# Two attentions of a fused two-layer block: the mixes of the key tiles one chunk sooner on TensorE, and their copy on ScalarE behind chunk 3

## The chip, the cores and the metric

One core of one Trainium2 chip runs the whole program in one launch. The metric is the time of an execution on the device in microseconds, as the median of several runs.

## What is computed

The reference is a block of two layers on x of shape (8, 512, 128). Each layer normalises x and adds an attention and a feed-forward branch to it. The change touches only the two attentions, which have 16 heads of 8 dimensions and a causal mask:

```
scores = q @ k^T            (layer 0: q_cos k_cos + q_sin k_sin, scaled by a factor of the head)
scores = where(causal mask, scores, -inf)
attn   = softmax(scores, axis=-1)
out    = (attn @ v) @ Wo.T
```

## The kernel before

The program runs in phases: setup, mix0, middle0, attend0, middle1, experts1, attend1. attend0 and attend1 are the same function, `attend` (line 1863 on), with layer 0 or 1.

**Units.** The work of an attention is cut into 32 units: 8 batches (called rows) by 4 groups of 4 heads. A unit is one batch's 512 queries against its 512 keys for 4 heads. The causal mask leaves four key tiles of 128 (kt 0 to 3) with 512, 384, 256 and 128 queries each.

**Steps.** Each engine has a program of its own and walks through steps t = 0, 1, 2, ... (`in_steps`). In step t TensorE has in hand:
- unit t: `maxima`, the scores with queries on the partitions, from which VectorE takes each query's maximum (`reduce`);
- unit t-1: `turn_maxima`, which turns the maxima round, so that VectorE can copy them (`copy_maxima`) and SyncE's DMA can put them into q as extra rows;
- unit t-2: `probabilities`, the scores with keys on the partitions, less the maximum, which ScalarE takes to exponentials (`exponentials`, line 2089) and GpSimd masks on the diagonal (`mask`, line 2052);
- unit t-3: `mix` (line 2176), the exponentials times the values. It runs once for each key tile in the order 0, 1, 3, 2, with 4 heads side by side as 32 columns each of the array (shape 128*32), and adds up in one bank, MIX. ScalarE copies the bank to mixT (line 2114);
- unit t-4: `turn_mix` (line 2184), which turns mixT in four pieces of 128*128 into the bank TURN, from where VectorE divides by the sums (`divide`, lines 2287 and 2291) into context.

A step has five chunks, c = 0 to 4, because the scores of a unit fill five pairs of banks. In each chunk TensorE issues the probabilities of side 0, the maxima, and the probabilities of side 1; all three use the array as two halves of 64 partitions (shapes 50*128, 48*128 and 64*128). The probabilities have one bank a side: those of chunk c wait until ScalarE has taken the exponentials of chunk c-1 of that side. `maxima` has two pairs of banks and waits for the reduction two chunks back.

**What stands between the chunks on TensorE.** After chunk 0 `turn_mix`. After chunk 1 the mix of tile 0 and `turn_maxima`, which waits for the divided context, since both use the bank TURN. After chunk 2 the mix of tile 1. After chunk 3 the mixes of tiles 3 and 2. When the unit t-4 was the last of a row, there are also `turn_context` after chunk 2 (line 2190) and `project` after chunk 4 (line 2196), the copy of the turned context on ScalarE after chunk 3's exponentials (line 2102), and the sum into x on VectorE (`add_row`, lines 2304 and 2308), for which the next `turn_mix` waits.

**Other engines.** ScalarE's step is the ten exponentials in order, then the copy of the mix. VectorE's step is `split_maxima` of unit t-1 (lines 2271 and 2273), then the five reductions (lines 2255, 2258, 2260, 2261) with `divide` after the first and `copy_maxima` after the second. GpSimd gathers rows by DMA, copies the values (line 2060) and masks. In attention 0 it also has the second norm of the other branch, with products at lines 2022, 2027 and 2031, and in attention 1 the additions at line 2041. In attention 0 the norm adds statistics on VectorE in one step of four and four activations on ScalarE (line 2107) in the next. The order is written out by hand in the `step` functions, and semaphores carry the waits.

## Time and profile before

| | us |
|---|---|
| median of 3 runs | 1272.88 |
| lowest and highest of them | 1272.55, 1272.88 |
| the profiled execution | 1268.47 |
| its span | 1266.9 |
| busy TensorE (matmul), share of the span | 981.7, 77% |
| busy VectorE | 819.4, 65% |
| busy ScalarE | 690.9, 55% |
| busy GpSimd | 582.5, 46% |
| line 2089, exponentials, 640 of 600 ns | 351.1 |
| line 2176, mixes, 2048 instructions | 178.9 |

The profile records one execution. A row of its timeline has the start from the beginning of the span, the length, the engine, the line of the kernel, the operation, what is written and read, the shapes, and in brackets the idle time in front of it with the instruction that ended it. PE is TensorE, PEld its weight loads, ACT ScalarE, DVE VectorE, POOL GpSimd. Rows that follow on each other with the same form are merged (x4). A matmul's length has a tail that overlaps with the next one, so distances between starts tell more than lengths do. Attention 0 runs from about 395 to 660 us of the span, and attention 1 from about 1000 to its end.

### The profile page before, as it was taken

To read this page: it belongs to the slowest core of one execution; us is meant where nothing else is said; L and a number is where in the kernel's file an instruction comes from. 1 tells how busy PE (TensorE), PEld (TensorE's weight loads), DVE (VectorE), ACT (ScalarE), POOL (GpSimd) and SP (SyncE) were. 2 spreads that over 40 slices of the span, in tenths; PEclk is the share of its full clock that TensorE was granted. 3 is DMA by queue.
4 is the path that set the end of the run, shared out by engine and by line. 5 is a ranking of instruction groups with operands and counts; after the bars stand their busy time and mean duration, and the time that the engine had idled before them with its cause. 6 is when DMAs were issued, how large, how long until landed. Compare 5 with 4: busy or idle time off the path is not lost. (4 is left out here: it accounts for less than half of the span.)

```text
span 1266.9 us, 27743 instructions
## 1 busy us (share of the span) xinstructions
PE 981.7 (77%) x8908; PEld 647.1 (51%) x8908; DVE 819.4 (65%) x1770; ACT 690.9 (55%) x1325; POOL 582.5 (46%) x793
## 2 busy tenths in 40 slices
PE   3789652989867988888872655199999599999987
PEld 1456431777753544444431433188888345555553
DVE  1566341667748999999943776133333699999992
ACT  1366343878714777677763454022222277777775
POOL 3467537010112565565551466411110367777775
PEclk9899776999985999999996666599999599999999
DMA  4321042577752222222201434456665112211111
GB/s 134 108 51 51 26 118 74 160 210 225 208 172 77 80 69 69 72 76 62 73 24 36 115 115 119 142 164 194 185 192 163 39 46 54 55 52 51 51 45 30
DMA packets 151735, 126.30 MB, mean 100 GB/s; under 512 B 23760, under 2 KB 134272, under 8 KB 151648
## 3 DMA queue, kind: packets, MB, share of 16 engines
q1 hardware_dynamic: 141904, 107.05, 29.5%
q0 software_dynamic: 8016, 17.71, 4.8%
q8 instruction: 44, 0.72, 0.2%
q10 hardware_dynamic: 1728, 0.46, 0.2%
q14 instruction: 43, 0.35, 0.1%
HBM read 77.83 MB, written 44.70 MB: 97 GB/s over the span
## 5 line engine op out<-in xcount | busy, mean ns | idle before, releaser
L2089 ACT ACTIVATE attend_probs<-attend_attend_ps 128x512 f32<-128x512 f32 x640 | 351.1, 600 | 161.7 <-PE attend_attend_ps L2163 154.4
L2163 PE MATMUL attend_attend_ps<-attend_q,attend_ks 50*128 50x512 f16 (+3 forms) x1024 | 236.5, 307 | 20.1 <-ACT attend_probs L2089 18.0
L2052 POOL TENSOR_SCALAR_AFFINE_SELECT attend_probs<-attend_probs 128x512 f32<-128x512 f32 x256 | 158.7, 637 | 159.5 <-ACT attend_probs L2089 158.6
L2131 PE MATMUL attend_attend_ps<-attend_ks,attend_q 48*128 48x512 f16 (+3 forms) x1024 | 191.3, 317 | 25.5 <-DMA attend_ks<-k_stack 16.2
L2176 PE MATMUL attend_attend_ps<-attend_probs,attend_vals 128*32 128x512 f32 (+3 forms) x2048 | 178.9, 446 | 0.0
L2258 DVE TENSOR_REDUCE attend_neg_max<-attend_attend_ps 128x2 f32<-128x1024 f32 x128 | 155.0, 1211 | 9.9 <-PE attend_attend_ps L2143 9.8
L2143 PE MATMUL attend_attend_ps<-identb,stairs 64*128 64x128 bf16 (+1 forms) x1280 | 144.3, 213 | 0.0
L2163 PEld LDWEIGHTS attend_attend_ps<-attend_q,attend_ks 50*128 50x128 f16 x1024 | 70.9, 94 | 116.1 <-ACT attend_probs L2089 93.2
L2260 DVE TENSOR_REDUCE attend_neg_max<-attend_attend_ps 128x2 f32<-128x768 f32 x128 | 121.8, 951 | 9.2 <-PE attend_attend_ps L2143 8.4
L1800 DVE TENSOR_TENSOR experts_hidden<-experts_experts_ps,experts_gate 128x512 f32<-128x512 f32 x39 | 27.0, 691 | 136.3 <-ACT experts_gate L1779 136.3
L2143 PEld LDWEIGHTS attend_attend_ps<-identb,stairs 64*128 64x128 bf16 x1280 | 105.9, 100 | 17.5 <-issue 4.7
L1834 PE MATMUL experts_experts_ps<-experts_rowsT,experts_w_in 128*128 128x256 f32 (+1 forms) x468 | 110.1, 385 | 1.6 <-ACT experts_rowsT L1787 1.5
L1104 POOL DMA_INDIRECT sorted<-middle_scaled,rank_row x64 | 66.6, 1040 | 58.1 <-issue 28.9
L1834 PEld LDWEIGHTS experts_experts_ps<-experts_rowsT,experts_w_in 128*128 128x128 f32 (+1 forms) x468 | 82.4, 183 | 17.6 <-ACT experts_rowsT L1787 2.1
L1779 ACT ACTIVATE experts_gate<-experts_experts_ps 128x512 f32<-128x512 f32 x39 | 23.3, 597 | 120.8 <-PE experts_experts_ps L1834 120.8
L1766 POOL DMA_DIRECT2D experts_rows<-sorted x39 | 27.7, 712 | 131.8 <-issue 131.8
L2131 PEld LDWEIGHTS attend_attend_ps<-attend_ks,attend_q 48*128 48x128 f16 x1024 | 67.2, 96 | 39.0 <-DMA attend_ks<-k_stack 16.6
L2255 DVE TENSOR_REDUCE attend_neg_max<-attend_attend_ps 128x4 f32<-128x1024 f32 x64 | 78.3, 1224 | 8.5 <-PE attend_attend_ps L2143 8.5
L1430 POOL TENSOR_TENSOR x_sum<-middle_amp_n,middle_sine 128x1024 f32<-128x1024 f32 x8 | 18.9, 2365 | 118.4 <-DVE middle_amp_n L1636 118.3
L2068 POOL DMA_INDIRECT attend_moe<-done,back_row x64 | 61.6, 962 | 14.9 <-issue 14.9
L1846 PE MATMUL experts_experts_ps<-experts_w_out,experts_hidden 128*128 128x128 f32 (+1 forms) x468 | 58.7, 275 | 0.9 <-DVE experts_result L1811 0.9
L2176 PEld LDWEIGHTS attend_attend_ps<-attend_probs,attend_vals 128*32 128x32 f32 x2048 | 44.7, 109 | 22.8 <-issue 5.9
(319 smaller groups left out, 1950.7 us busy)
## 6 DMA issues: line engine op xcount, KB each, us to landing
experts_w_in<-in_L_ffn_w_dram SPq DMA_DIRECT2D x78, 176.0 KB, 2.4
q_stack<-middle_parts SPq DMA_DIRECT2D x24, 256.0 KB, 3.3
k_stack<-middle_parts SPq DMA_DIRECT2D x24, 256.0 KB, 3.6
attend_q<-q_stack SPq DMA_DIRECT2D x64, 96.0 KB, 2.2
attend_ks<-k_stack SPq DMA_DIRECT2D x64, 96.0 KB, 2.2
middle_w_in<-in_L_ffn_W_dram SPq DMA_DIRECT2D x23, 256.0 KB, 2.7
middle_w_out<-in_L_ffn_W_dram SPq DMA_DIRECT2D x23, 256.0 KB, 3.1
experts_rows<-sorted POOLq DMA_DIRECT2D x39, 128.0 KB, 2.5
```

The source lines that it names most:

```text
L1104: pool.indirect_dma_start(k.sorted1, bass.IndirectOffsetOnAxis(ap=k.rank_row[:, c * NT + tile:c * NT + tile + 1], axis=0), scaled[:, c, ti ...
L1834: mm = pe.matmul(ps[0:size[c], hidden_bank(u, bank), half * ROWS:(half + 1) * ROWS], w_in[:, u.phase, w + c * P:w + c * P + size[c]], rows ...
L2052: pool.affine_select(out=block_, in_=block_, compare_op=ALU.is_ge, fill=0.0, base=0, pattern=[[0, GH], [1, P]], channel_multiplier=-1).the ...
L2068: pool.indirect_dma_start(moe[:, c * NT + n, :], None, src, bass.IndirectOffsetOnAxis(ap=at_row[:, c * NT + n:c * NT + n + 1], axis=0))\
L2089: act.activation(probs[:, u.par, 2 * c + side, :], ps[:, PROB + side, :], ACT.Exp, scale=SCALE ** -2)\
L2131: pe.matmul(ps[:, bank + side, col:col + (qt + 1) * P], q[rows(side, KR), g, pair, qt * P:(qt + 1) * P], ks[rows(side, KR), g, pair, 0:(qt ...
L2143: mm = pe.matmul(span[:, :, col:col + 64], k.stairs[here, stair:stair + P], k.identb[here, here].unsqueeze(1).broadcast_to([64, len(blocks ...
L2163: mm = pe.matmul(ps[:, PROB + side, col:col + S - kt * P], ks[rows(side, KM), g, pair, kt * P:(kt + 1) * P], q[rows(side, KM), g, pair, kt ...
L2176: mm = pe.matmul(ps[32 * h:32 * h + 32, MIX, kt * P:S], vals[:, u.par, kt * GH + h, :], probs[:, u.par, 2 * c + h % 2, col:col + S - kt * ...
L2255: ins = dve.tensor_reduce(out[:, :, :, 1], pair_banks.rearrange("p s (h t) -> p s h t", h=HP), X_AXIS, ALU.max, negate=True)
L2258: ins = dve.tensor_reduce(out[:, :, c // 2, 3], pair_banks, X_AXIS, ALU.max, negate=True)
L2260: dve.tensor_reduce(out[:, :, c // 2, 2], pair_banks[:, :, 0:384], X_AXIS, ALU.max, negate=True)
```

## The change

On TensorE the mix of tile 0 moves from behind chunk 1 to behind chunk 0, ahead of `turn_mix`. The mix of tile 1 moves from behind chunk 2 to behind chunk 1, ahead of `turn_maxima`, and those of tiles 3 and 2 move from behind chunk 3 to behind chunk 2, ahead of `turn_context`. On ScalarE the copy of the mix moves from the end of the step to behind chunk 3's exponentials, ahead of the copy of the turned context and of chunk 4's exponentials. Its waits are the same. The number of instructions is the same.

```diff
--- before.py
+++ after.py
@@ -2095,6 +2095,12 @@
                     if active(t, 2, UNITS):
                         for side in range(2):
                             exponentials(t - 2, c, side)
+                    if c == 3 and active(t, 3, UNITS):
+                        u = t - 3
+                        act.wait_ge(mixed.sem, mixed.done(u))
+                        if u.past(1):
+                            act.wait_ge(mix_turned.sem, mix_turned.done(u - 1))
+                        act.copy(mixT[:, :], ps[:, MIX, :]).then_inc(mixT_ready.sem, 1)
                     if c == 3 and row_ends:
                         r = (t - 4).row
                         act.wait_ge(context_turned.sem, context_turned.done(r))
@@ -2106,12 +2112,6 @@
                         for j in range(QT):
                             act.activation(z_norm[:, j, :], z_sum[:, j, :], ACT.Identity, bias=z_shift[:, j:j + 1],
                                            scale=z_rstd[:, j:j + 1]).then_inc(z_normed.sem, 1)
-                if active(t, 3, UNITS):
-                    u = t - 3
-                    act.wait_ge(mixed.sem, mixed.done(u))
-                    if u.past(1):
-                        act.wait_ge(mix_turned.sem, mix_turned.done(u - 1))
-                    act.copy(mixT[:, :], ps[:, MIX, :]).then_inc(mixT_ready.sem, 1)
 
             in_steps(act, UNITS, DEPTH + 1 - layer, step, 2 * NG, 2 * NG)
 
@@ -2222,13 +2222,13 @@
                         maxima(t, c)
                     if active(t, 2, UNITS):
                         probabilities(t - 2, c, 1)
+                    if active(t, 3, UNITS) and c <= 2:
+                        mix(t - 3, c)
+                        if c == 2:
+                            mix(t - 3, 3)
                     if c == 0 and active(t, 4, UNITS):
                         before_mix(t)
                         turn_mix(t - 4)
-                    if 1 <= c <= 3 and active(t, 3, UNITS):
-                        mix(t - 3, c - 1)
-                        if c == 3:
-                            mix(t - 3, 3)
                     if c == 1 and active(t, 1, UNITS):
                         before_maxima(t)
                         turn_maxima(t - 1)
```

## Rows read from the trace of the kernel before

**Rows 1.** Windows, attention 0: us, then PE, PEld, DVE, ACT, POOL busy; clock; DMA.
```profile
411.00:640.00 229.00, 199.09 (x2553) 109.11 (x2548) 218.11 (x401) 173.54 (x336) 132.81 (x196) 1.00 0.25 70
```

**Rows 2.** Timeline of TensorE, attention 1, one step: start us, length us.
```profile
1120.43 0.33 PE L2163 MATMUL attend_attend_ps<-attend_q,attend_ks 50*128 50x384 f16 x1
...
1121.10 0.86 PE L2176 MATMUL attend_attend_ps<-attend_probs,attend_vals 128*32 128x128 f32 x16
1121.89 0.28 PE L2163 MATMUL attend_attend_ps<-attend_q,attend_ks 50*128 50x256 f16 x1
...
1122.96 0.39 PE L2163 MATMUL attend_attend_ps<-attend_q,attend_ks 50*128 50x512 f16 x1 [0.34 <-ACT attend_probs L2089]
...
1123.45 0.39 PE L2163 MATMUL attend_attend_ps<-attend_q,attend_ks 50*128 50x512 f16 x1
1124.02 0.63 PE L2184 MATMUL attend_attend_ps<-ident,attend_mixT 128*128 128x128 f32 x4 [0.18 <-ACT attend_mixT L2114]
1124.58 0.39 PE L2163 MATMUL attend_attend_ps<-attend_q,attend_ks 50*128 50x512 f16 x1
...
1124.93 0.38 PE L2163 MATMUL attend_attend_ps<-attend_q,attend_ks 50*128 50x512 f16 x1
...
1125.24 1.07 PE L2176 MATMUL attend_attend_ps<-attend_probs,attend_vals 128*32 128x512 f32 x8
1126.12 0.22 PE L2151 MATMUL attend_attend_ps<-identh,attend_max_parts 128*32 128x128 f16 x1
1126.27 0.33 PE L2163 MATMUL attend_attend_ps<-attend_q,attend_ks 50*128 50x384 f16 x1
...
1126.88 0.85 PE L2176 MATMUL attend_attend_ps<-attend_probs,attend_vals 128*32 128x384 f32 x8
1127.67 0.33 PE L2163 MATMUL attend_attend_ps<-attend_q,attend_ks 50*128 50x384 f16 x1
```

**Rows 3.** Timeline of ScalarE, attention 1: the same step.
```profile
1122.31 1.09 ACT L2089 ACTIVATE attend_probs<-attend_attend_ps 128x512 f32<-128x512 f32 x2 [0.37 <-PE attend_attend_ps L2163]
1123.28 0.59 ACT L2114 COPY attend_mixT<-attend_attend_ps 128x512 f32<-128x512 f32 x1
1123.75 2.34 ACT L2089 ACTIVATE attend_probs<-attend_attend_ps 128x512 f32<-128x512 f32 x4
```

**Rows 4.** Timeline of ScalarE, attention 1: further copies of the mix.
```profile
1106.44 0.59 ACT L2114 COPY attend_mixT<-attend_attend_ps 128x512 f32<-128x512 f32 x1
...
1115.22 0.61 ACT L2114 COPY attend_mixT<-attend_attend_ps 128x512 f32<-128x512 f32 x1
...
1130.52 0.59 ACT L2114 COPY attend_mixT<-attend_attend_ps 128x512 f32<-128x512 f32 x1
```

**Rows 5.** Timeline of ScalarE, attention 0: copies of the mix.
```profile
548.68 0.59 ACT L2114 COPY attend_mixT<-attend_attend_ps 128x512 f32<-128x512 f32 x1
...
557.72 0.59 ACT L2114 COPY attend_mixT<-attend_attend_ps 128x512 f32<-128x512 f32 x1
...
565.92 0.59 ACT L2114 COPY attend_mixT<-attend_attend_ps 128x512 f32<-128x512 f32 x1
```

**Rows 6.** Timeline of VectorE, attention 0, beside GpSimd.
```profile
558.60 1.20 DVE L2273 SCALAR_TENSOR_TENSOR attend_max_parts<-attend_neg_max,attend_max_parts 128x16 f16<-128x16 f32 x1
...
561.14 0.29 DVE L2291 TENSOR_TENSOR attend_context<-attend_attend_ps,attend_inv 128x128 f32<-128x128 f32 x1
```

**Rows 7.** Timeline of GpSimd, attention 0, at that moment.
```profile
558.50 1.27 POOL L2027 TENSOR_TENSOR attend_z_gain<-attend_z_norm,row 128x512 f32<-128x512 f32 x1
```

**Rows 8.** Timeline of TensorE, attention 0, a step that ends a row.
```profile
536.50 0.85 PE L2176 MATMUL attend_attend_ps<-attend_probs,attend_vals 128*32 128x384 f32 x8
537.28 0.66 PE L2190 MATMUL attend_attend_ps<-ident,attend_context 128*128 128x128 f32 x4
...
539.98 1.16 PE L2196 MATMUL attend_attend_ps<-wT,attend_contextT 128*128 128x128 f32 x8
```

**Rows 9.** Waits, attention 0, 450 to 630 us: total us, times, longest us.
```profile
PE attend_attend_ps L2151 <- DVE attend_context L2291: 14.8, 14, 1.4
```

## Prediction

> **What bounds the kernel now.** I read four views in this order: the windows, to see which engine is full in the attentions; TensorE's timeline of one step, to see what follows what; ScalarE's timeline of the same step, to see what TensorE waits for; and then the copies of the mix (line 2114, one a step), whose distances are the lengths of the steps. The change touches both attentions and nothing else, so only the 31 steps of each in which score matmuls and mixes run together count.
>
> In attention 0 VectorE is busy 218.11 of 229.00 us, 95%, at a granted TensorE clock of 1.00, full speed [rows 1]. That looks like the bound. TensorE's timeline says that it is only a near neighbour. Call the start of chunk 3's first probability matmul zero (1120.43). Then chunk 4's comes at 1.46, the next step's chunk 0 at 2.53, its second side at 3.02, the turning of the mix at 3.59, chunk 1 at 4.15 and its second side at 4.50, mix of key tile 0 at 4.81, the turning of the maxima at 5.69, chunk 2 at 5.84, the second mix at 6.45 and zero again at 7.24 [rows 2]. Two places in this line are waits. Chunk 0 stands 0.34 idle for an exponential, and the turning of the mix stands 0.18 idle for the copy of the mix. Everywhere else one piece of TensorE follows on another.
>
> ScalarE's side of it [rows 3]: chunk 4's first exponential starts at 1122.31, which is 0.42 after its matmul (1121.89), and chunk 0's matmul (1122.96) starts 0.65 after that exponential. So each side needs 0.42 + 0.65 = 1.07 us for a chunk, whatever TensorE's load is, since each side has one bank. Two exponentials take 0.97 (to the copy at 1123.28) and the copy holds back what is behind it by 0.47 (1123.75). One loop sets the step: TensorE's pieces from chunk 0's second side to chunk 4, and then the round trip over ScalarE.
>
> The steps' lengths: an ordinary one takes 7.24 (1123.28 to 1130.52), the one after a row's last unit 8.06 (1115.22 to 1123.28), the one into it in attention 1 8.78 (1106.44 to 1115.22) [rows 3, 4]. In attention 0 two steps of each row are long, 9.04 and 8.20 [rows 5]. In the 8.20 step VectorE's second half of the split maxima takes 1.20 and ends at 559.80, 0.03 after a GpSimd product that runs from 558.50 to 559.77, and the context is only there at 561.43 [rows 6, 7].
>
> **The edit on ScalarE.** The copy moves from behind chunk 4 to behind chunk 3. Its own wait, for the mix, costs nothing, because the last mix now stands ahead of chunk 3's probability matmuls on TensorE. Behind it in ScalarE's queue stand chunk 4's exponentials. Chunk 3's first exponential starts at 0.42, the copy at 0.42 + 0.97 = 1.39, chunk 4's exponentials at 1.86 and 2.35, and so chunk 0's matmuls at 1.86 + 0.65 = 2.51 and 3.00. Before they came at 2.53 and 3.02. The 0.79 us of the last two mixes that leave chunk 3 (1121.10 to 1121.89 [rows 2]) therefore buy nothing: what they occupied, the copy and the round trip of 1.07 now occupy. At the other end the copy is done long before the turning of the mix, which removes the wait of 0.18 there.
>
> **The edit on TensorE.** At 3.00 the old order had 0.57 to the turning of the mix. The new one puts the first mix there. The steps of the sum:
> - second side of chunk 0 to the mix: 0.31, as chunk 1's second side to the mix now (1124.93 to 1125.24); mix at 3.31.
> - mix of key tile 0: 0.88 to the turning of the maxima (1125.24 to 1126.12), which has the mix's shape (128*32). Leaving for another shape costs more: the second mix has 384 columns of 512, three quarters, which of 0.88 is 0.66, and takes 0.79 to chunk 3's matmul [rows 2]. So a change of shape is an estimated 0.13. The same 384-column mix takes 0.78 to the turning of the context [rows 8], so turning counts as another shape, and the first mix costs 0.88 + 0.13 = 1.01 here. Turning of the mix at 4.32, chunk 1 0.56 later at 4.88.
> - chunk 1 takes 0.66 to its mix (1124.58 to 1125.24), the second mix 0.66 because the maxima are turned behind it, and these 0.15: chunk 2 at 6.35.
> - chunk 2 takes 0.61, the last two mixes 0.79: zero again at 7.75.
>
> The ordinary step goes from 7.24 to 7.75, **+0.51**. Put shortly: one mix piece enters chunk 0 where only 0.26 was slack, and what leaves chunk 3 was covered. The change of shapes saved is in this sum: from mix to turning is still a change of shape, so of eight changes a step seven are left, and it gives 0.13. The Trainium skill, "TensorEngine Tiling (Array Packing)", Key Properties, says that changing the tiling mode drains TensorE; with the 0.13 the trace agrees. Read as the thing that bounds the step, that rule would make the edit a gain, and the rows' price for it is rival (a).
>
> VectorE can follow, since its work stays the same, 95% of the old steps' time, and the steps get longer. The turning of the maxima waits for the divided context. With the mix turned at about 4.9 and 0.6 for the division (0.29 is its second half [rows 6]), it is there at 5.5, before 6.20.
>
> **The step behind a row's last unit.** ScalarE now has two copies in chunk 3: mix at 1.39, context at 1.86, ready at 2.45. The projection starts at 2.5 and takes 1.1 (1.16 with its tail [rows 8]), so chunk 0 starts at 3.6. Then 0.66 to the mix, 1.01, 0.56, 0.66, 0.66, 0.15, 0.61, 0.79: 8.70 against 8.06, **+0.64**. The turning used to wait there for VectorE's addition to the row; the first mix now covers that, and it is in the sum.
>
> **The long steps.** In the 8.20 step TensorE waits for the context at 561.43. The copy at 557.72 is 2.85 behind zero (1123.28 less 1120.43), so the context is at 6.56. The work that delays it hangs on chunk 4's last exponential, which does not move (2.35 against 2.36). New and old order both stand at 6.56 there, and 0.08 + 0.15 + 0.61 + 0.79 more give 8.2: **+0.0**. The 8.78 step is of this kind plus the turned context, and gains or loses nothing either. The 9.04 step waits for the context too: TensorE stood 14.8 us in 14 such waits, up to 1.4 each, in 180 us [rows 9]. There the masks come late, and the first mix may stand for one at chunk 0. I bound this step by −0.1 and +0.5 and take 0, since the long wait covers it.
>
> **Sum.** Attention 0, a row of four steps: 0.51 + 0.64 = 1.15. Attention 1: 2 × 0.51 + 0.64 = 1.66. Seven full rows each give 8.1 + 11.6 = 19.7, and the three steps at either attention's edges, at an estimated 0.3 each, 1.8: together +21.5. The profiled execution took 1268.47, with a span of 1266.9, so its successor would take 1290. The median of the runs, 1272.88, lies 4.4 above it; forecast **1294**.
>
> **Rivals.**
> (a) Faster. The ordinary step loses a change of shape (0.13) and the wait of 0.18 at the turning, and the first mix runs in the shadow of the exponentials. Then some 46 steps of the 62 that are not held by the context gain 0.31: −14, 1259. It decides at chunk 0: its second side must then be issued some 0.5 earlier than now. For it: the 0.13 itself, and two waits that go. Against: the copy in chunk 3 keeps chunk 0 at 2.51. Chance 0.06.
> (b) Nothing measurable. The wait for the context, which hides the edit in the 8.20 step, hides it everywhere; VectorE's 95% speaks for it in attention 0, and the missing wait ahead of the maxima's turning at 1126.12 against it in attention 1. About 1273. Chance 0.07.
> (c) Much slower, by a new collision. The division follows the turning that now comes 0.7 later, and VectorE's small operations fall on other GpSimd work. One took 1.20 [rows 6]. One more such collision per row, at the whole of it, is 16 × 1.2 = 19 on top: 1313. It decides if a division or a split meets a product that it misses now. The Trainium skill, "SBUF — State Buffer", Who interferes with whom, says that the loser of the shared ports blocks until the other instruction has finished; the 0.03 us between the two ends agrees. Chance 0.10.
> (d) The forecast's own mechanism, 0.77. That the edit does nothing can't be: both queues' orders change.
>
> Within 0.2% of the median (2.5 us, about what a measurement of this kernel tells from none) lies only (b): same 0.07, faster 0.06, slower 0.77 + 0.10 = 0.87. If attention 0 hides all of its 9.0 us and attention 1 pays two thirds of its 12.5, the time is about 1281; (c) but for its last microsecond gives the upper end. Range 1279 to 1312.
>
> **What would show it.** Right: the copy of the mix 1.4 behind chunk 3's start, chunk 4's exponential straight behind it with no idle time, chunk 0's matmuls at 2.5 and 3.0, about 1.0 from first mix to turning, ordinary steps of 7.7 to 7.8 and the 8.20 steps unchanged. Wrong: ordinary steps under 7.3, chunk 0 before 2.2, or a mix that waits on masks in ordinary steps.

## Result and profile after

The changed kernel takes 1302.29 us, the median of 5 runs (1300.51 to 1304.25), against 1272.59 for the kernel before beside it (5 runs, 1271.64 to 1272.88): a ratio of 1.0237, 95% interval 1.0223 to 1.0251, slower by 30 us. Forecast were 1294 in a range of 1279 to 1312. The profiled execution took 1302.29 as well; that of the kernel before, 1268.47, is faster than all five of its runs, so the two profiles differ by more than the medians do.

The profile's page, part 1: the span and the engines' busy time.

```profile
span 1300.7 us, 27743 instructions
...
PE 1005.9 (77%) x8908; PEld 654.7 (50%) x8908; DVE 830.5 (64%) x1770; ACT 690.5 (53%) x1325; POOL 582.0 (45%) x793
```

The instruction counts are those of before. The span has grown by 33.8 us, from 1266.9. TensorE's busy time grew with it by 24 us (from 981.7), and that has to be explained, since the work is the same.

TensorE's timeline in an ordinary step of attention 1, to be laid beside [rows 2]. Columns: start, length, engine, line, operation, idle time in front.

```profile
1152.99 0.33 PE L2163 MATMUL attend_attend_ps<-attend_q,attend_ks 50*128 50x384 f16 x1
...
1154.07 0.28 PE L2163 MATMUL attend_attend_ps<-attend_q,attend_ks 50*128 50x256 f16 x1 [0.34 <-ACT attend_probs L2089]
...
1155.54 0.39 PE L2163 MATMUL attend_attend_ps<-attend_q,attend_ks 50*128 50x512 f16 x1 [0.59 <-ACT attend_probs L2089]
...
1156.03 0.39 PE L2163 MATMUL attend_attend_ps<-attend_q,attend_ks 50*128 50x512 f16 x1
1156.35 1.07 PE L2176 MATMUL attend_attend_ps<-attend_probs,attend_vals 128*32 128x512 f32 x8
1157.34 0.66 PE L2184 MATMUL attend_attend_ps<-ident,attend_mixT 128*128 128x128 f32 x4
1157.93 0.39 PE L2163 MATMUL attend_attend_ps<-attend_q,attend_ks 50*128 50x512 f16 x1
...
1158.59 0.85 PE L2176 MATMUL attend_attend_ps<-attend_probs,attend_vals 128*32 128x384 f32 x8
1159.26 0.22 PE L2151 MATMUL attend_attend_ps<-identh,attend_max_parts 128*32 128x128 f16 x1
1159.41 0.33 PE L2163 MATMUL attend_attend_ps<-attend_q,attend_ks 50*128 50x384 f16 x1
...
1160.02 0.86 PE L2176 MATMUL attend_attend_ps<-attend_probs,attend_vals 128*32 128x128 f32 x16
1160.81 0.33 PE L2163 MATMUL attend_attend_ps<-attend_q,attend_ks 50*128 50x384 f16 x1
```

Zero of the prediction, chunk 3's first probability matmul, is at 1152.99. Counted from there: chunk 4 at 1.08, chunk 0 at 2.55 and its second side at 3.04, the first mix at 3.36, the turning at 4.35, chunk 1 at 4.94, the second mix at 5.60, the turning of the maxima at 6.27, chunk 2 at 6.42, the last mixes at 7.03, zero again at 7.82. The prediction had 1.07, 2.51, 3.00, 3.31, 4.32, 4.88, 5.54, 6.20, 6.35, 6.96 and 7.75. Two places now are long waits for exponentials, 0.34 at chunk 4 and 0.59 at chunk 0. The waits for the copy and behind it are gone, and between chunk 0 and chunk 3 TensorE never waits.

ScalarE in the same step, beside [rows 3].

```profile
1153.42 1.08 ACT L2089 ACTIVATE attend_probs<-attend_attend_ps 128x512 f32<-128x512 f32 x2 [0.31 <-PE attend_attend_ps L2163]
1154.39 0.59 ACT L2103 COPY attend_mixT<-attend_attend_ps 128x512 f32<-128x512 f32 x1
1154.86 2.19 ACT L2089 ACTIVATE attend_probs<-attend_attend_ps 128x512 f32<-128x512 f32 x4
...
1162.20 0.59 ACT L2103 COPY attend_mixT<-attend_attend_ps 128x512 f32<-128x512 f32 x1
```

The copy starts 1.40 after zero (1154.39), chunk 4's first exponential straight behind it at 1154.86, and the next copy comes 7.81 later. This is the ordinary step, 7.24 before.

The steps' lengths, as distances of the copies (attention 0 unless said otherwise; "behind" and "into" leave out the edges of the attentions):

| step | before | after | forecast |
|---|---|---|---|
| ordinary | 7.24 | 7.82 | 7.75 |
| into the row's last unit, attention 0 | 7.82 | 8.40 | as ordinary, +0.51 |
| behind a row's last unit, attention 1 | 7.86 to 8.06, mostly 7.98 to 8.02 | 8.68 | 8.70 |
| behind a row's last unit, attention 0 | 7.87 to 7.97; 10.07 and 9.76 at the start of two turns of the loop | 8.68; 10.75 and 8.68 there | 8.70 |
| with the norm's activations | 9.02 to 9.12 | 9.05 to 9.07, twice 10.56 | 9.04 |
| with GpSimd's products | 8.20 | 8.21, twice 9.33 | 8.20 |
| into the last unit, attention 1 | 8.78 | 8.81 | 8.78 |

From the first copy to the last, attention 0 takes 267.5 us where it took 250.9, and attention 1 252.0 where it took 236.1. These 32.4 us are all but 1.4 of the span's growth. The last distance of attention 0 alone grew from 3.72 to 5.46, at a clock of 0.69; the kernel before has the same in its second trace (5.41 at 0.68, further down), so the change is not its cause.

The 9.07 step kept its length because its wait for the context absorbed the first mix. TensorE at the turning of the maxima in it, in the kernel before and in the changed one:

```profile
485.12 0.23 PE L2151 MATMUL attend_attend_ps<-identh,attend_max_parts 128*32 128x128 f16 x1 [1.36 <-DVE attend_context L2291]
```

```profile
490.46 0.23 PE L2151 MATMUL attend_attend_ps<-identh,attend_max_parts 128*32 128x128 f16 x1 [0.32 <-DVE attend_context L2291]
```

Of 1.36 us of waiting 0.32 are left. Ahead of the first mix TensorE now waits 0.19 for a mask, as the prediction had thought possible.

What the forecast lacked are above all the steps of 10.56 and 9.33. The windows of the changed kernel, with these steps as stretches: us, busy PE, PEld, DVE, ACT, POOL, then TensorE's granted clock.

```profile
520.96:531.52 10.56, 9.39 (x93) 4.25 (x91) 9.13 (x19) 7.32 (x16) 5.53 (x9) 0.74 0.27 76
531.52:540.85 9.33, 8.39 (x93) 4.08 (x90) 8.41 (x13) 5.90 (x12) 6.26 (x8) 0.82 0.20 57
557.93:568.49 10.56, 8.92 (x94) 4.13 (x91) 9.14 (x19) 7.38 (x17) 5.53 (x9) 0.84 0.28 76
...
593.78:602.85 9.07, 7.60 (x94) 3.75 (x91) 8.93 (x19) 7.32 (x16) 5.56 (x9) 1.00 0.31 88
```

The long steps have a mean clock of 0.74, 0.82 and 0.84; an undisturbed 9.07 step (the last row) has 1.00. Between 411 and 650 us of the span the mean is 0.96, where the kernel before has 1.00 ([rows 1], to 640 us). TensorE's timeline in the third of these steps shows the lower of the two levels, 1.2 GHz in place of 2.4, in the instructions' lengths.

```profile
559.08 0.39 PE L2163 MATMUL attend_attend_ps<-attend_q,attend_ks 50*128 50x512 f16 x1 [0.59 <-ACT attend_probs L2089]
...
560.42 1.83 PE L2176 MATMUL attend_attend_ps<-attend_probs,attend_vals 128*32 128x512 f32 x8 [0.17 <-POOL attend_probs L2052]
562.19 1.11 PE L2184 MATMUL attend_attend_ps<-ident,attend_mixT 128*128 128x128 f32 x4
```

The first mix takes 1.83 where it takes 1.07 in the ordinary step, and the turning 1.11 in place of 0.66. Part of TensorE's additional busy time is there. The granted clock in this step is 1.00 up to 560 us and 0.50 from 561 to 564. Just before it fell, TensorE had stood 0.34 us for chunk 4's exponential (557.61) and 0.59 for chunk 0's (559.08), 0.9 us together, where it stands 0.34 in the kernel before. It is so at nearly every fall: this trace and a second one of the changed kernel (below) have eleven falls before the last distances of the attentions, and ten of them come right behind such a wait of 0.59 to 0.68 us in chunk 0, at most 1.5 us after it. The eleventh, between 519 and 520 us, came behind a wait of 1.59 us for the context (517.72); the kernel before waits 1.41 at the same place (511.15) and keeps 1.00. Idle time added up over a step does not explain it: the norm's step of the kernel before has TensorE busy for 7.07 of 9.05 us, that of the changed kernel for 7.57 of 9.07.

### The profile page after: what moved, and what is told of

It is laid out like the page before. It is cut to its first block and busy times, and to the rows that moved or that the text cites. A ratio compares the mean times of both kernels' runs of the same rounds, so it can differ in the third digit from the quotient of the medians.

```text
span 1300.7 us, 27743 instructions
## 1 busy us (share of the span) xinstructions
PE 1005.9 (77%) x8908; PEld 654.7 (50%) x8908; DVE 830.5 (64%) x1770; ACT 690.5 (53%) x1325; POOL 582.0 (45%) x793
## 5 line engine op out<-in xcount | busy, mean ns | idle before, releaser
L2163 PE MATMUL attend_attend_ps<-attend_q,attend_ks 50*128 50x512 f16 (+3 forms) x1024 | 241.1, 309 | 54.1 <-ACT attend_probs L2089 51.3
L2131 PE MATMUL attend_attend_ps<-attend_ks,attend_q 48*128 48x384 f16 (+3 forms) x1024 | 187.8, 317 | 24.5 <-DMA attend_ks<-k_stack 16.3
L2176 PE MATMUL attend_attend_ps<-attend_probs,attend_vals 128*32 128x512 f32 (+3 forms) x2048 | 184.9, 457 | 1.2 <-POOL attend_probs L2052 0.9
L2143 PE MATMUL attend_attend_ps<-identb,stairs 64*128 64x128 bf16 (+1 forms) x1280 | 140.7, 214 | 0.0
L2143 PEld LDWEIGHTS attend_attend_ps<-identb,stairs 64*128 64x128 bf16 x1280 | 102.0, 100 | 19.2 <-issue 5.0
L2131 PEld LDWEIGHTS attend_attend_ps<-attend_ks,attend_q 48*128 48x128 f16 x1024 | 63.5, 96 | 37.4 <-DMA attend_ks<-k_stack 16.7
```

The source lines that it names most:

```text
L2131: pe.matmul(ps[:, bank + side, col:col + (qt + 1) * P], q[rows(side, KR), g, pair, qt * P:(qt + 1) * P], ks[rows(side, KR), g, pair, 0:(qt ...
L2143: mm = pe.matmul(span[:, :, col:col + 64], k.stairs[here, stair:stair + P], k.identb[here, here].unsqueeze(1).broadcast_to([64, len(blocks ...
L2163: mm = pe.matmul(ps[:, PROB + side, col:col + S - kt * P], ks[rows(side, KM), g, pair, kt * P:(kt + 1) * P], q[rows(side, KM), g, pair, kt ...
L2176: mm = pe.matmul(ps[32 * h:32 * h + 32, MIX, kt * P:S], vals[:, u.par, kt * GH + h, :], probs[:, u.par, 2 * c + h % 2, col:col + S - kt * ...
```

## Experiments

Each kernel was compared with the kernel before on its own chip, so ratios carry over from one group to the next and medians don't.

### One edit at a time

Only ScalarE's edit:

```diff
@@ scalar, step(t)
+                    if c == 3 and active(t, 3, UNITS):
+                        ...
+                        act.copy(mixT[:, :], ps[:, MIX, :]).then_inc(mixT_ready.sem, 1)
...
-                if active(t, 3, UNITS):
-                    ...
-                    act.copy(mixT[:, :], ps[:, MIX, :]).then_inc(mixT_ready.sem, 1)
```

> Only ScalarE's edit is made: the copy of the mix stands behind chunk 3's exponentials, the mixes stay behind chunks 1, 2 and 3. The round-trip theory: the copy now has to wait for the mixes behind chunk 3 and starts about 1.65 us after the chunk's start, so chunk 4's exponential comes at 2.13 in place of 1.88 and chunk 0 of the next step 0.25 later; but the 0.26 us in which the turning of the mix waited for the copy go, so an ordinary step stays at 7.24 (7.2 to 7.3). In the step that ends a row the copy of the context slips behind the copy of the mix, the projection starts some 0.7 later, and the 8.06 steps become 8.6 to 8.8. Sum about +9 us, 1280 to 1284. The rival, that the early copy is what costs in the changed kernel, wants ordinary steps of 7.6 and over, and 1290 or more.

Ratio 1.014 (1.0104 to 1.0176). TensorE in an ordinary step of attention 0, where zero is 421.14:

```profile
421.14 0.33 PE L2163 MATMUL attend_attend_ps<-attend_q,attend_ks 50*128 50x384 f16 x1
...
423.95 0.37 PE L2163 MATMUL attend_attend_ps<-attend_q,attend_ks 50*128 50x512 f16 x1 [0.63 <-ACT attend_probs L2089]
...
424.68 0.65 PE L2184 MATMUL attend_attend_ps<-ident,attend_mixT 128*128 128x128 f32 x4
...
425.92 1.06 PE L2176 MATMUL attend_attend_ps<-attend_probs,attend_vals 128*32 128x512 f32 x8
426.94 0.23 PE L2151 MATMUL attend_attend_ps<-identh,attend_max_parts 128*32 128x128 f16 x1
```

Chunk 0 is at 2.81 and the turning at 3.54 (2.53 and 3.59 before), as the walk had it, with no wait at the turning. The step is 7.36 and not 7.24, because the turning of the maxima now starts 1.02 behind the first mix, not 0.88. The cause is VectorE's split of the maxima: its first half starts at 424.72, takes 0.31 and ends 0.02 behind GpSimd's last mask (424.37 and 0.64 long), and the reduction and the division stand behind it. In the steps behind a row's last unit the expected 8.6 to 8.8 came out as 8.56. Attention 0 as a whole takes 255.5 from first to last copy, 4.6 more than before, about half of the 9 that were expected of both attentions together. Its 8.20 steps rose to 8.40, which was not expected, and the 9.76 step behind a row's last unit fell to 8.73. No full step of attention 0 is at the lower clock.

In the group of these first four experiments attention 1 was slow in every kernel, in steps that end a row above all (10.2 us and more), and the kernel before took 1292.04 beside them. All four ratios are larger than expected (+18, +30, +18 and -11 us, where +9, +14 to +18, +8 to +14 and -2 to -5 were forecast). So I read their ratios for the sign, and the steps in attention 0 alone. The traces show one part of the slowness: with only ScalarE's edit the steps behind a row's last unit in attention 1 take 11.1 to 11.3 us at a clock of 0.69 to 0.70. What made the steps of 10.2 was not found; in the next group they were gone, on the same chip.

Only TensorE's edit:

```diff
@@ tensor, step(t)
+                    if active(t, 3, UNITS) and c <= 2:
+                        mix(t - 3, c)
+                        if c == 2:
+                            mix(t - 3, 3)
                     if c == 0 and active(t, 4, UNITS):
                         before_mix(t)
                         turn_mix(t - 4)
-                    if 1 <= c <= 3 and active(t, 3, UNITS):
-                        mix(t - 3, c - 1)
-                        if c == 3:
-                            mix(t - 3, 3)
```

> Only TensorE's edit is made: the mixes stand behind chunks 0, 1 and 2, the copy stays at the end of ScalarE's step. The round-trip theory: chunk 4's exponential comes at 1.49 after chunk 3's start, chunk 0 at 2.14 and 2.63, but the first mix then waits for the copy of the mix before (one bank), which ends at 3.07, and starts at 3.17. Ordinary steps of 7.63 to 7.70, the 8.06 steps 8.3, the 8.20 and 8.78 steps as before: 1286 to 1290. The rival, that fewer changes of shape on TensorE are worth something by themselves, wants ordinary steps at or under 7.24.

Ratio 1.0234 (1.0204 to 1.0264).

```profile
423.43 0.33 PE L2163 MATMUL attend_attend_ps<-attend_q,attend_ks 50*128 50x384 f16 x1
...
424.51 0.28 PE L2163 MATMUL attend_attend_ps<-attend_q,attend_ks 50*128 50x256 f16 x1 [0.35 <-ACT attend_probs L2089]
...
425.68 0.37 PE L2163 MATMUL attend_attend_ps<-attend_q,attend_ks 50*128 50x512 f16 x1 [0.29 <-ACT attend_probs L2089]
...
426.64 1.07 PE L2176 MATMUL attend_attend_ps<-attend_probs,attend_vals 128*32 128x512 f32 x8 [0.17 <-ACT attend_mixT L2114]
...
431.11 0.33 PE L2163 MATMUL attend_attend_ps<-attend_q,attend_ks 50*128 50x384 f16 x1
```

From zero at 423.43, chunk 4 is at 1.08, chunk 0 at 2.25, the first mix at 3.21 after an idle 0.17 for the copy, which is the one-bank wait of the expectation. The step is 7.68 (copies 7.67 apart). The steps behind a row's last unit came out as 7.85 and not 8.3, for which I had not walked through the earlier chunk 0. Those into a row's last unit rose by more than the ordinary ones, from 7.82 to 8.60, and the 8.20 steps fell to 7.95, where no change was expected; both stayed unexplained. TensorE's edit makes +0.43 of an ordinary step, ScalarE's +0.12, both +0.58. The rival, that fewer changes of shape are a gain, falls here. Chunk 0 at 2.25 also shows what the copy does in the changed kernel: with it behind chunk 3, chunk 0 comes at 2.55. This trace has two full steps of attention 0 at the lower clock (10.42 at 0.84 and 9.25 at 0.82) and one at its end (9.90 at 0.83); that of ScalarE's edit has none.

### Is the place that the last mixes leave worth anything?

```diff
-                    if 1 <= c <= 3 and active(t, 3, UNITS):
+                    if 1 <= c <= 2 and active(t, 3, UNITS):
                         mix(t - 3, c - 1)
-                        if c == 3:
+                        if c == 2:
+                            mix(t - 3, 2)
                             mix(t - 3, 3)
```

> Of the change only one part: the last two mixes go from behind chunk 3 to behind chunk 2, where the second mix already stands, so TensorE has one piece of mixes fewer per step, and the copy stays at the step's end. The round-trip theory: 0.66 us of mixes come in where TensorE is the bound and only 0.39 come out, since chunk 4 cannot start before 1.07 after chunk 3: ordinary steps +0.27 or, if the turning still waits for its copy, a little less, 7.45 to 7.55; in all 1280 to 1286. The rival, that each change of shape saved is a gain, wants -0.13 per step and 1265.

Ratio 1.0136 (1.0102 to 1.017); ordinary steps of 7.59, 0.04 more than the top of the expectation.

```profile
422.84 1.50 PE L2176 MATMUL attend_attend_ps<-attend_probs,attend_vals 128*32 128x384 f32 x24
424.27 0.33 PE L2163 MATMUL attend_attend_ps<-attend_q,attend_ks 50*128 50x384 f16 x1
...
425.35 0.28 PE L2163 MATMUL attend_attend_ps<-attend_q,attend_ks 50*128 50x256 f16 x1 [0.34 <-ACT attend_probs L2089]
...
426.52 0.37 PE L2163 MATMUL attend_attend_ps<-attend_q,attend_ks 50*128 50x512 f16 x1 [0.29 <-ACT attend_probs L2089]
```

The mixes of chunk 2 take 1.43 to chunk 3 (422.84 to 424.27), 0.64 more than one alone, and chunk 4 comes 1.08 behind chunk 3 where it came 1.46 behind it. So 0.64 come in and 0.38 go out; 0.10 more come in because chunk 0 now follows chunk 4 by 1.17 and not by 1.07. Together they make the 0.35 of the step. One piece of mixes less per step is a loss. It is the round trip over ScalarE, 1.08, that sets the distance of these chunks once TensorE has less to do than that.

The other direction, the last mix in chunk 4:

```diff
                     if 1 <= c <= 3 and active(t, 3, UNITS):
                         mix(t - 3, c - 1)
-                        if c == 3:
-                            mix(t - 3, 3)
+                    if c == (3 if row_ends else 4) and active(t, 3, UNITS):
+                        mix(t - 3, 3)
```

> The opposite direction: the last mix (256 columns) goes one chunk later, from behind chunk 3 to behind chunk 4, where TensorE stands idle for 0.34 us, except in the steps that end a row. One more change of shape per step. The round-trip theory: TensorE's own line would allow 6.9 us; VectorE, which needs about 7.07 of the 7.24, becomes the bound, so ordinary steps of 7.07 to 7.15, the others unchanged: -2 to -5 us, 1268 to 1271. The rival, that a change of shape costs more than the place gives, wants ordinary steps of 7.3 and over.

Ratio 0.9912 (0.9884 to 0.994).

```profile
423.45 0.33 PE L2163 MATMUL attend_attend_ps<-attend_q,attend_ks 50*128 50x384 f16 x1
...
425.34 0.64 PE L2176 MATMUL attend_attend_ps<-attend_probs,attend_vals 128*32 128x256 f32 x8
425.91 0.39 PE L2163 MATMUL attend_attend_ps<-attend_q,attend_ks 50*128 50x512 f16 x1
...
430.55 0.33 PE L2163 MATMUL attend_attend_ps<-attend_q,attend_ks 50*128 50x384 f16 x1
```

The mix (425.34) lies in what was idle time, chunk 0 comes 2.46 behind zero (423.45) in place of 2.53, and zero again at 7.10. Ordinary steps are 7.09 apart. With this mix gone from chunk 3, chunk 4 comes 1.08 behind chunk 3 (424.53) and not 1.46, and the mix then fills the time to chunk 0. A change of shape more per step, and it is faster: what counts is where the piece stands. The steps behind a row's last unit fell too, to 7.7, and the 8.20 steps to 7.92, which I had not expected.

### The long steps

The prediction let the change cost nothing where VectorE's context is late because of GpSimd's products. VectorE in such a step of the changed kernel, attention 1:

```profile
1164.06 0.46 DVE L2271 TENSOR_SCALAR attend_max_parts<-attend_neg_max 128x16 f16<-128x16 f32 x1
1164.55 1.21 DVE L2273 SCALAR_TENSOR_TENSOR attend_max_parts<-attend_neg_max,attend_max_parts 128x16 f16<-128x16 f32 x1
...
1167.10 0.29 DVE L2291 TENSOR_TENSOR attend_context<-attend_attend_ps,attend_inv 128x128 f32<-128x128 f32 x1
```

The split's second half takes 1.21, the context is there at 1167.39, and TensorE turns the maxima at 1167.44. The split's first half takes 0.46 (0.19 in the kernel before, and in e5 below): GpSimd's last mask (1163.86, 0.64 long) now runs when VectorE comes to it, as in the kernel with ScalarE's edit alone.

GpSimd's products spread over successive steps, on the kernel before and on the changed one:

```diff
@@ gpsimd
                 if n < UNITS:
-                    for i in range(QT):
-                        mask(n, i)
-                if layer == 0 and n >= 7 and (n - 7) % NG == 0:
-                    second_gain((n - 7) // NG)
-                if layer == 1 and n >= NG and n % NG == 0:
-                    join_branches(n // NG - 1)
+                    mask(n, 0)
+                if layer == 0 and n >= 7 and (n - 7) % NG == 0:
+                    second_scale((n - 7) // NG)
+                if layer == 0 and n >= 8 and (n % NG == 0 or n == UNITS + NG - 1):
+                    second_shift(n // NG - 2 + (n % NG) // 3)
+                if layer == 1 and n >= 3 and n % NG != 2 and n <= UNITS + 1:
+                    join_branches((n - 3) // NG, (n - 3) % NG)
+                if n < UNITS:
+                    for i in range(1, QT):
+                        mask(n, i)
```

second_scale and second_shift are the two products of second_gain, and join_branches does one of its three additions per call; only the second and the third wait for the gathered rows.

> The kernel before once more, for its trace on the same chip as the other runs of this call. Ordinary steps of 7.24 in both attentions, the steps that meet GpSimd's products 8.20 in attention 0 and 8.78 in attention 1. If the chip of the first call alone was slower in attention 1, these hold here; if it is this chip too, the extra time shows in the step into a row's last unit of attention 1, which took 10.2 us and more in all four runs of that call.

The profiled execution took 1268.28; both expectations of the first kind hold: 7.23, 8.19 to 8.20 and 8.78 to 8.80. Its steps are those of the first trace to 0.02 us nearly everywhere; the largest exception is the last distance of attention 0, 5.41 at a clock of 0.68 in place of 3.72 at 1.00.

> The kernel before with GpSimd's row work (two products of the norm in attention 0, three additions in attention 1) taken from behind the masks and put one at a time behind the first mask of successive steps, where GpSimd stands idle. Theory of the long steps: VectorE's split maxima wait for a GpSimd product to end, the context is late by a microsecond, and TensorE waits for it. Then the 8.20 steps fall to 7.24 and the 8.78 steps to 7.8, some 15 of them: 1256 to 1260. Rival: the long steps are long for their own TensorE work, and stay as they are: 1272.

Median 1256.50, ratio 0.988 (0.9857 to 0.9902). VectorE and GpSimd where the 8.20 step was:

```profile
558.21 0.19 DVE L2277 TENSOR_SCALAR attend_max_parts<-attend_neg_max 128x16 f16<-128x16 f32 x1
558.43 0.20 DVE L2279 SCALAR_TENSOR_TENSOR attend_max_parts<-attend_neg_max,attend_max_parts 128x16 f16<-128x16 f32 x1
...
559.97 0.29 DVE L2297 TENSOR_TENSOR attend_context<-attend_attend_ps,attend_inv 128x128 f32<-128x128 f32 x1
```

```profile
553.50 1.29 POOL L2027 TENSOR_TENSOR attend_z_gain<-attend_z_norm,row 128x512 f32<-128x512 f32 x1
...
558.32 0.29 POOL L2062 COPY attend_vals<-v_all 128x128 f32<-128x128 f32 x1
...
561.03 1.28 POOL L2033 TENSOR_TENSOR attend_z_tile<-attend_z_gain,row 128x512 f32<-128x512 f32 x1
```

The products stand in GpSimd's idle time (553.50, 561.03), the split's halves take 0.19 and 0.20, and the step is 7.23. In attention 1 all 8.78 steps are 7.82. So the 8.20 and 8.78 steps were long by the wait for a GpSimd product, and it could be had back without touching TensorE. The 9.04 steps stay at 9.02 to 9.11: their late context has another cause, which no run isolated. One step at the end of attention 0 is at the lower clock here too (8.32 at 0.79, where the kernel before has 7.86).

> The changed kernel with the same GpSimd work spread. If the wait for the context hides the change's 0.59 us in the 8.20 and 8.78 steps, they become 7.8 and 8.4 here, no lower, and the distance to the kernel before with the same spread (e5) is larger than that of the changed kernel to the kernel before: about 0.55 us in each of the 15 steps more, 8 us. The changed kernel gains only some 6 us from the spread: 1294 to 1298. Rival: the change costs nothing in these steps for another reason, and both kernels gain the same 15 us.

Median 1298.66, ratio 1.0234 (1.0204 to 1.0265) to the kernel before. The steps are 7.80 and 8.40, no lower. Against e5 the distance is 42 us, where 30 lie between the two original kernels. Of the 12 more, 15 steps of 0.58 are 9. The rest may be steps at the lower clock, of which this trace has six (9.33, 10.57, 10.73 and 10.28 in attention 0, 9.97 and 9.99 in attention 1), but that was not separated. So the change does cost its 0.58 in each of these steps as soon as their cover is taken away. The 6 us that the changed kernel itself was to gain from the spread do not show: its ratio is 1.0234 with it and 1.0237 without.

### The lower clock

> The changed kernel once more beside the one with the filler, on the same chip: some 1300 to 1304 where the kernel before takes 1271 to 1273; one to five steps in its trace that are over a microsecond longer than the others of their kind, each in a stretch at the lower granted clock, and at other places than in the first trace.

Median 1304.83 (6 runs), ratio 1.026 (1.023 to 1.0291). The trace has six such long steps in attention 0, one more than expected. Three are the same steps as in the first trace (the two that follow the first step of the loop's second turn, and the norm's step of the next row), three are others. The window over attention 0:

```profile
411.00:650.00 239.00, 206.65 (x2475) 109.97 (x2475) 218.19 (x391) 169.19 (x329) 130.72 (x193) 0.96 0.24 67
```

> The changed kernel with two matmuls of 512 columns more in chunk 4 of each step but those that end a row, into the bank TURN, which nobody reads at that time. They fall into the time in which TensorE waits for chunk 4's exponentials (0.59 us idle, 0.43 us of work), so ordinary steps stay at 7.82, at most 7.9. Theory of the rest of the loss: the steps of 9.3 and 10.6 us are steps at the lower TensorE clock, granted after TensorE had stood idle more than in the kernel before; with the filler the granted clock is 1.00 through both attentions, those steps are 8.2 and 9.07, and the time falls by 3 to 6 us against the changed kernel. Rival: the long steps come from GpSimd or DMA, and stay.

```diff
                     if c == 4 and row_ends:
                         project(t - 4)
+                    elif c == 4 and active(t, 2, UNITS) and active(t, 1, UNITS):
+                        pe.wait_ge(maxT_ready.sem, maxT_ready.done(t - 1))
+                        for _ in range(2):
+                            pe.matmul(ps[:, TURN, :], k.identb[:, :], k.stairs[:, 0:128].unsqueeze(1).broadcast_to([P, 4, P]),
+                                      start=True, stop=True)
```

Ratio 1.0254 (1.0228 to 1.028): no gain in time, but not for the rival's reason. All steps with the norm are 9.05 to 9.07, all with the products 8.21 to 8.22, ordinary ones stay at 7.82, and each of them is at 1.00. But two steps behind a row's last unit took 14.20 and 14.56. The window of such a step and TensorE in it:

```profile
503.00:518.00 15.00, 10.99 (x110) 5.74 (x109) 9.85 (x15) 6.88 (x13) 4.33 (x6) 0.77 0.15 40
```

```profile
505.49 1.16 PE L2196 MATMUL attend_attend_ps<-wT,attend_contextT 128*128 128x128 f32 x8 [0.58 <-ACT attend_contextT L2108]
509.63 0.60 PE L2163 MATMUL attend_attend_ps<-attend_q,attend_ks 50*128 50x512 f16 x1 [2.98 <-issue]
```

TensorE stands 2.98 us before chunk 0 ("issue": the profile shows nothing that it waited for), and then the clock falls. It happened at the start of two turns of the loop over 8 steps. The same steps take 10.07 and 9.76 in the kernel before, at full clock, and 10.75 and 8.68 in the changed one. The DMA view has a likely cause: between 500 and 650 us the instruction queue moves 18 transfers (0.29 MB) here, three of them at each of the two stalls (505 to 511 and 579 to 585), and one in that stretch in the kernel before, in the changed one and in the next experiment's. The other twelve fall where nothing stalls, so this is likely and not shown: TensorE waited for its instructions, and no row names that as the releaser. With this, the run does not tell whether the filler would gain time without the stalls.

> The changed kernel with one matmul of 512 columns more (0.21 us) in chunk 4 of two steps of four, those before the 9.07 and the 8.20 step, in attention 0 alone. The larger filler kept the clock up in these steps, but TensorE stood 3 us without a cause that the profile shows at the start of two turns of the loop, and lost the gain. If that came from the 48 instructions more in a turn of the loop, it is gone here with 8 more: long step behind a row's end back at 10.5 to 10.8, the 10.56 and 9.33 steps gone or rarer, and 1297 to 1301, 2 to 5 us under the changed kernel. If one small matmul is too little to hold the clock, the lower clock shows in some of these steps and the time is that of the changed kernel, 1301 to 1305.

The diff is that of e8 with `layer == 0 and t.group in (0, 1)` in the condition and one matmul. Median 1298.70, ratio 1.0213 (1.0196 to 1.0231). Over attention 0:

```profile
411.00:650.00 239.00, 210.25 (x2531) 112.52 (x2527) 222.66 (x398) 171.76 (x334) 133.30 (x197) 0.99 0.23 67
```

The clock there is 0.99, one step of the norm's kind is still disturbed (10.12 at 0.76) and one takes 9.26 at full clock, the others are 9.05 to 9.07, and all steps with products 8.21 to 8.23. A step at the end of attention 0, where no filler runs, is at 0.83 (10.06). The steps behind a row's end are back at 11.01 and 10.27. In attention 1, which has no filler here, two steps are at the lower clock (9.40 and 8.96). Against the changed kernel's 1.0237 and 1.026 that is 3 to 6 us less, for two more matmuls per row and nothing moved; the intervals overlap by a hair, so the size is not sure. Of the norm's and the products' steps in attention 0 four are at the lower clock in the changed kernel's first trace and four in its second, one here and none with the larger filler. That speaks for the theory that work in TensorE's idle time keeps the clock up, and so does the place of the falls, right behind that idle time. With one trace for each kernel, and falls that differ between executions, it is supported and not settled.

### A kernel that beats both

> The products spread and the last mix behind chunk 4, both on the kernel before. If the two gains are of different steps they add up: ordinary steps at VectorE's bound of 7.09, the long ones with them, 1248 to 1253. Rival: with GpSimd's products moved, other collisions take their place and it stays above 1257.

Both edits, e4's and e5's, on the kernel before: median 1248.39, ratio 0.9816 (0.9796 to 0.9836). The gains add up. Former 8.20 steps are 6.97, ordinary ones of attention 1 6.97 as well, and no full step of either attention in its trace is at the lower clock; the last two distances of attention 0 are (8.02 at 0.91 and 5.94 at 0.55). Ordinary steps were expected at 7.09; only the first three of each attention have that.

## Why the prediction was right

**The mechanism** was right in each part. Chunk 0 stayed where it was (2.55; forecast 2.51, before 2.53), because the copy took the place that the last mixes left. Without the copy there (only TensorE's edit), chunk 0 comes at 2.25. And where the last mixes alone move, chunk 4 comes earlier, but by 0.38 and not by the 0.64 put in elsewhere. The first mix entered a line of TensorE that had 0.26 to spare. It costs 0.99 to the turning (1156.35 to 1157.34), where the sum had 1.01, made of 0.88 and an estimated 0.13 for the change of shape.

**The ordinary step** was forecast at +0.51 and is +0.58. Of the 0.07, 0.05 are there by the first mix (the walk's latencies, each a hundredth or two short), 0.02 go again because the mix takes 0.99 and not 1.01, 0.03 are the turning's, which takes 0.59 to chunk 1 behind a mix and 0.56 where it had waited, and 0.01 comes later.

**The step behind a row's last unit** was forecast at 8.70 and is 8.68. Its cost was not +0.64, though: the 8.06 from which the prediction started is the longest of its kind in attention 1, most are 7.98 to 8.02, and the step costs about 0.70. **The long steps** were forecast at no change and are 8.21, 8.81 and 9.07 wherever the clock stayed. For the first two the cause given, a context late by a GpSimd product, was shown by spreading the products: the changed kernel then pays in them too. For the 9.07 step the wait that shrank from 1.36 to 0.32 shows that the context covered the cost.

**What the sum lacked.** On the profiled executions it gave +21.5, and +33.8 were measured; between the medians it is +29.7. The ordinary kind was counted 21 times in the fourteen rows, at 0.07 more each: 1.5. The first three steps of each attention cost 0.59 and not 0.3: 1.7. Four steps at the lower clock in attention 0 cost 1.5, 1.5, 1.1 and 1.1, and one at the end of attention 1 cost 1.3 (8.94, where the changed kernel's second trace has 7.61): 6.5. With these it is 31.2; some 2.6 are left over, 1.4 of them outside the stretches from first to last copy. The other 1.2 are the balance of larger terms: +1.7 from the last distance of attention 0, which the kernel before has in one of its two traces; +0.8 from the steps behind a row's last unit; +1.3 from two steps at the edges of attention 0 (8.42 to 9.06 and 7.86 to 8.51, forecast as unchanged); and -2.5 from two steps that got shorter (9.76 to 8.68 and 8.34 to 8.20) where +0.64 each was forecast.

The largest error is thus a term that was not there: the prediction took the clock of 1.00 in the old trace as given, and put the price of TensorE's longer idle time in chunks 3, 4 and 0 at nothing. That the falls of the clock cost 6.5 us is read from the steps; that the idle time brings them on is supported by the place of the falls and by the two fillers, and not settled. The range held in part by luck: the change cost 8 us more than the forecast, and the upper end of 1312 had been priced for a collision on VectorE, rival (c), which did not come about in that size. No term of it was for the clock.

**The rivals.** (a), that fewer changes of shape pay, is refuted by three experiments: one change of shape fewer made the kernel slower twice (1.0234 and 1.0136), and one more made it faster (0.9912). (b) holds in the steps held by the context and nowhere else. Of (c) a small part happened: the split's first half meets the last mask and takes 0.46 in place of 0.19; it costs time only where the context is the last to arrive, as with ScalarE's edit alone.

## What to carry to other kernels

Before moving work out of a busy stretch, ask what else fixes that stretch's length. Here a round trip of 1.07 us per bank did, and it took in the copy and gave nothing back. A piece belongs where the engine would wait anyway, as the last mix in chunk 4. It takes 0.57 there (425.34 to 425.91), more than the old wait of 0.34, but its leaving chunk 3 had made room. Walk one period of the trace with starts only, each row against its releaser; that gave the ordinary step and the one behind a row's last unit to 0.1 us. But take the length of a kind of step from several of that kind, not from one. Then look at a step that is longer than its neighbours: the cheapest gain in this kernel was in GpSimd's products, which the change does not touch. And a matmul added to fill idle time makes the loop longer, which can cost more than it gives: look at the instruction queue in the DMA view.

## What the runs showed of the hardware

- TensorE's granted clock fell from 2.4 to 1.2 GHz for single stretches of the changed kernel (0.50 from 561 to 564 us; mean 0.74 to 0.84 of a step) although the engine does not stand long there: ten of eleven falls came right behind a wait of 0.59 to 0.68 us in chunk 0, which follows one of 0.20 to 0.66 in chunk 4. The eleventh came behind a wait of 1.59. The kernel before, with waits of 0.34 and 0.18 in an ordinary step and up to 1.41 in others, kept 1.00 in every full step of both attentions in two traces; in one of them the last distance of attention 0 was at 0.68. At which step it falls differs in part from one execution to the next. The changed kernel's runs beside the larger filler spread over 11 us (1298.06 to 1309.02), but those of the kernel before there spread over 8.5 as well, so the spread is no evidence for it.
- A small VectorE operation on tiles outside the matmul banks (128x16) ends 0.02 to 0.03 us after the GpSimd instruction that runs when it would have ended: 0.17 us alone (1147.84 and 1148.04 in the trace before), 1.20 beside a product, 0.46 beside a mask. The reductions, which read the banks, take 1.21 beside a product too (559.73). Nothing of this shows as a wait; it is busy time of VectorE.
- With two more matmuls in six of eight steps of TensorE's loop, the instruction queue made 18 transfers (0.29 MB) between 500 and 650 us, where the kernel before and the changed one made one, and TensorE stood 2.98 and 2.92 us without a recorded cause at the start of two turns.
- Leaving the mix's shape for another costs TensorE 0.12 us: a mix of 384 columns takes 0.67 to the turning of the maxima (1158.59 to 1159.26) and 0.79 to probabilities [rows 2].
